# The prologue of an attention kernel rearranged: first batch's norm and queries alone, the mask loaded earlier, K's third part in halves

## The chip, the cores and the metric

The kernel runs on one core of one Trainium2 chip. The metric is the device time of one execution in microseconds, the median of several runs of the same program.

## What is computed

One transformer-like block over two batches of 256 query tokens of width 256: cross attention onto 4096 context keys (16 heads of 16), then a retention layer, then a small mixture of experts, each with a residual. Only the start of the cross attention matters here:

```python
q = split_heads(layernorm(x) @ w_q.T + b_q)          # 2 x 256 queries, 16 heads x 16
k = split_heads(ctx @ w_k.T + b_k)                   # 2 x 4096 keys
v = split_heads(ctx @ w_v.T + b_v)
scores = einsum('bhqd,bhkd->bhqk', q, k) / 4
scores = where(mask, -inf, scores)                   # mask: 1x1x256x4096, the same for both batches
attn = einsum('bhqk,bhkd->bhqd', softmax(scores), v)
x1 = x + attn @ w_o.T + b_o
```

The mask hides all but the last 896 keys or so, plus a part of the first block of these. The kernel works on these 7 blocks of 128 keys (`KB`), and checks from the whole mask that nothing else is shown. If something is, a general path with a loop over windows runs; it does not run with these inputs.

## The kernel before

**Precision by parts.** Queries and keys are float32, each split into three bfloat16 parts (high, middle, low): `hi = bf16(v)`, `rest = v - hi`, `mid = bf16(rest)`, `low = rest - mid`. Six products of parts (`K_PART`, `Q_PART`) stand below one another in the contraction: `kstack` and `qstack` have 6 x 16 = 96 rows for each head. They are filled by DMAs from SBUF to SBUF, six for each piece: three of K's high part, two of its middle, one of its low part and so for the queries, in another order. Rows 96 to 98 (`MROW:KROWS`) hold ones in `kstack` and the maximum, in three parts, in `qstack`, so that scores come out with the maximum subtracted. One DMA writes the ones, `kstack<-onesb` (L365), three rows of 57,344 bytes in pieces of 1,024.

**Pieces.** `n = 2b + f`: batch b, half f of the heads. `k0` to `k3` are K's four pieces of 128 x 896, `q` has the same four of 128 x 256. The kernel before makes the queries of both batches in one go (L589 to L598: transposes of four normed tiles, matmuls 512 columns wide).

**Stages and steps.** A stage is one batch and 4 heads (8 stages, `STAGES`). Each has 8 maximum tiles (`max_tile`, L656): a product of 128 queries and 896 keys on TensorE (L678, two halves, and L683 for the mask), whose maximum VectorE takes (L1461). Tiles use two pairs of PSUM banks in turn, so tile m waits until the maximum of tile m-2 is taken (`take_pair`). After a stage's 8th tile the maxima are split (L1480 to L1483), turned by TensorE (`turn_rows`, L699), copied by ScalarE (L1120) and loaded into `qstack` by a DMA. The main loop (`steps`) has 56 steps, 7 to a stage: `scores` (L724, two halves), exp on ScalarE (L1147), `weighted` sums (L740) of the step before; tiles of later stages are spread over the steps (`TILE_STEP`). The first `FIRST_TILES` = 10 tiles come before the loop.

**The prologue, engine by engine.** The order on each is written out by hand, and each engine takes its instructions strictly in order.

- SP issues loads: x (512 KB), w_k, the first batch's context in halves, w_q, w_v, then `kstack<-onesb`, then K's first piece and the middle and low parts of the first query piece to the stacks, then the two halves of the mask (512 KB each), the second context, and the other pieces.
- TensorE: 34 warm-up matmuls (68 records of L579), `keys(0)`, transposes, `queries()`, `keys(1)`, `values(0)`, `values(1)`; tile 0 (waits for `qstack` and `kstack`), `values(2)`, tile 1, `values(3)`, then tiles 2 to 9 with 3 warm-up matmuls behind each of tiles 2 to 6; `odd_late` (L995, sums of the late mask, behind tile 7); rows of stage 0; `odd_early` (L1001) with a last product of ScalarE's sums (L1004); `keys(2)`; the steps.
- VectorE: the norm of four tiles (L1366 to L1355), K(0)'s rest and its middle and low parts, the same for the first query piece, the rest of the second, the rest of K(1), and the maxima.
- ScalarE: evacuates PSUM (K's and the queries' high parts, the values), issues three `qstack` DMAs, sums the early mask (L1279: 3200 and 1600 columns), copies the rows, issues their DMA, forms the flag for the fast path (L1284, L1286) and copies K(2) in halves (L1100).
- GpSimd: constants, middle and low parts of the second queries (L490, L492), casts of the mask (L498, L499), K(1)'s low part (L503), then K(2) and K(3) in full (`keys_cut`: L516, L520, L524, L528).

## Time and profile before

| what | us |
|---|---|
| median of 3 runs | 248.17 (248.14 to 249.93) |
| the profiled execution, whole | 248.6 |
| its span (first to last instruction) | 246.8 |
| tile 0 starts | 26.34 |
| first scores (step 0) start | 43.15 |
| last of the 56 steps ends, about | 150 |

The profile is of one execution. Its times are microseconds from the start of its span. PE is TensorE's matmuls, PEld its weight loads, DVE VectorE, ACT ScalarE, POOL GpSimd, SP SyncE; a float32 matmul has two records. "Idle before" and the releaser behind "<-" say how long an engine stood before an instruction and what ended that. The granted clock of TensorE is given as a share of full speed, the DMA share as the mean busy share of the core's 16 DMA engines.

### The profile page before, as it was taken

The page shows a single profiled execution, that of the slowest core. Times are in us where ns is not written, and L with a number is a line of the kernel's source. Part 1 is how long each engine was busy: PE and PEld are TensorE (multiplying, and loading weights), DVE is VectorE, ACT ScalarE, POOL GpSimd, SP SyncE. Part 2 cuts the span into 40 slices and gives each one's busy share as a digit, 9 for nine tenths or more (in the row PEclk, how much of TensorE's full clock was granted, in tenths as well). Part 3 has the DMA queues.
Part 4 walks back from the last instruction along what each step waited for, and adds up shares of the span by engine and source line. Part 5 has one row for each costly group of instructions (what it writes and reads, how often), then busy time and mean ns, then how long its engine had stood idle before and what let it go on. Part 6 is the DMA issues. An engine that isn't in the chain of part 4 may idle for free.

```text
span 246.8 us, 3909 instructions
## 1 busy us (share of the span) xinstructions
PE 228.2 (92%) x1454; PEld 127.7 (52%) x1454; DVE 149.2 (60%) x340; ACT 111.6 (45%) x234; POOL 25.0 (10%) x28
## 2 busy tenths in 40 slices
PE   7979998999999999999999898989898889899892
PEld 7846684444565645454544433534746763635340
DVE  1656494893836748787876063485457538586682
ACT  2143463565747567777777784323144041201000
POOL 7002340805400400000000000000000000000000
PEclk9999999999999999999999999999999999999999
DMA  6659996909008800460000000000000000000000
GB/s 198 201 128 222 341 228 119 335 6 227 1 0 203 230 4 0 114 230 1 3 4 3 1 3 0 0 1 0 3 0 0 0 1 3 1 0 21 23 28 25
DMA packets 14541, 17.94 MB, mean 73 GB/s; under 512 B 2468, under 2 KB 13620, under 8 KB 14516
## 3 DMA queue, kind: packets, MB, share of 16 engines
q1 hardware_dynamic: 13220, 17.28, 25.5%
q10 hardware_dynamic: 1295, 0.34, 0.9%
q8 instruction: 14, 0.23, 0.4%
q14 instruction: 12, 0.09, 0.1%
HBM read 9.79 MB, written 0.52 MB: 42 GB/s over the span
## 4 chain that ended last, share of the span: by engine, by line
PE 70%; DVE 18%; ACT 5%; issue 3%; DMA 2%; SPq 0%; POOL 0%; DVEq 0%; ACTq 0%; POOLq 0%
PE bank L740 10%; PE bank L724 9%; PE bank L923 8%; PE bank L678 8%; DVE cneg L1461 7%; PE bank L830 6%; PE bank L579 4%; PE bank L633 4%; PE bank L640 4%; PE bank L903 3%; PE bank L791 3%; DMA qstack<-xbo 2%; ACT prob L1147 2%; PE bank L811 1%; PE bank L728 1%
## 5 line engine op out<-in xcount | busy, mean ns | idle before, releaser
L1461 DVE TENSOR_REDUCE cneg<-bank 128x1 f32<-128x896 f32 x64 | 68.2, 1088 | 33.1 <-PE bank L678 33.0
L1147 ACT ACTIVATE prob<-bank 128x512 f32<-128x512 f32 x112 | 65.6, 598 | 25.5 <-PE bank L724 17.0
L724 PE MATMUL bank<-qstack,kstack 99*128 99x256 bf16 x224 | 42.3, 274 | 1.7 <-ACT k_full L1100 0.8
L678 PE MATMUL bank<-kstack,qstack 96*128 96x448 bf16 x128 | 38.6, 354 | 0.8 <-DMA qstack<-xbo 0.4
L740 PE MATMUL bank<-prob,vals 128*32 128x256 f32 x448 | 35.8, 391 | 0.4 <-ACT prob L1147 0.4
L724 PEld LDWEIGHTS bank<-qstack,kstack 99*128 99x128 bf16 x224 | 17.5, 97 | 25.5 <-issue 12.1
L830 PE MATMUL bank<-w_late,xnT 128*128 128x512 f32 x48 | 22.0, 595 | 0.3 <-ACT xnT L1176 0.3
L678 PEld LDWEIGHTS bank<-kstack,qstack 96*128 96x128 bf16 x128 | 12.5, 98 | 9.6 <-DVE cneg L1461 1.7
L923 PE MATMUL bank<-ctxT,xnT 128*128 128x512 f32 x32 | 17.1, 616 | 0.3 <-DVE x_in L1641 0.3
L1641 DVE SCALAR_TENSOR_TENSOR x_in<-bank,nwts,x_in 128x256 f32<-128x256 f32 x32 | 15.5, 484 | 2.5 <-PE bank L923 1.4
L923 PE MATMUL bank<-kpart,xnT 128*128 128x512 f32 x32 | 16.3, 592 | 0.0
L740 PEld LDWEIGHTS bank<-prob,vals 128*32 128x32 f32 x448 | 8.8, 108 | 14.1 <-issue 11.1
L579 PE MATMUL bank<-ones 128*128 128x128 f32 x98 | 13.5, 297 | 1.5 <-POOL ones L481 1.4
L683 PE MATMUL bank<-hide_q,identb 128*128 128x128 bf16 x64 | 14.0, 219 | 0.0
L579 PEld LDWEIGHTS bank<-ones 128*128 128x128 f32 x98 | 13.1, 211 | 1.8 <-POOL ones L481 1.4
L640 PE MATMUL bank<-wv,ctxT 128*128 128x256 f32 x56 | 13.1, 383 | 0.2
L830 PEld LDWEIGHTS bank<-w_late,xnT 128*128 128x128 f32 x48 | 8.5, 190 | 8.2 <-issue 7.7
L633 PE MATMUL bank<-ctxT,wk 128*128 128x448 f32 x32 | 12.8, 542 | 0.0
L1176 ACT ACTIVATE xnT<-bank 128x256 f32<-128x256 f32 x8 | 3.0, 384 | 19.7 <-PE bank L791 19.7
L640 PEld LDWEIGHTS bank<-wv,ctxT 128*128 128x128 f32 x56 | 10.5, 190 | 2.3 <-DVE cneg L1461 0.7
L1500 DVE COPY acc<-bank 128x136 f32<-128x136 f32 x8 | 2.4, 299 | 13.0 <-PE bank L707 12.6
L923 PEld LDWEIGHTS bank<-kpart,xnT 128*128 128x128 f32 x32 | 6.1, 190 | 7.7 <-issue 7.7
(142 smaller groups left out, 260.4 us busy)
## 6 DMA issues: line engine op xcount, KB each, us to landing
kstack<-kpart SPq DMA_DIRECT2D x24, 224.0 KB, 4.5
w_late<-in_w_ret SPq DMA_DIRECT2D x1, 1536.0 KB
mask_all<-in_mask SPq DMA_DIRECT2D x2, 512.0 KB, 6.0
ctxT<-in_w_exp SPq DMA_DIRECT2D x1, 1024.0 KB
kpart<-in_w_exp SPq DMA_DIRECT2D x1, 1024.0 KB
ctxT<-in_ctxT SPq DMA_DIRECT2D x2, 448.0 KB, 6.2
ctxT<-in_ctxT SPq DMA_DIRECT2D x1, 896.0 KB, 9.4
qstack<-acc SPq DMA_DIRECT2D x6, 128.0 KB, 6.4
```

The costliest lines, as they stand in the source:

```text
L579: pe.matmul(bank[:, where, 0:P], ones[:, :], ones[:, :], start=True, stop=True)
L633: mm = pe.matmul(bank[:, banks + h, 0:HC], wk[:, i, f * P:(f + 1) * P], ctxT[:, b, i, h * HC:(h + 1) * HC], start=(i == 0), stop=(i == KIN ...
L640: mm = pe.matmul(out[:, (k - blocks[0]) * D:(k - blocks[0] + 1) * D], ctxT[:, b, i, k * P:(k + 1) * P], wv[:, i, :], start=(i == 0), stop= ...
L678: mm = pe.matmul(out, qstack[0:MROW, h, b, qt * P:(qt + 1) * P], kstack[0:MROW, b, h, half_ * HC:(half_ + 1) * HC], start=True, stop=not h ...
L683: pe.matmul(out[:, 0:P], identb[:, :], hide_q0[:, qt, :], start=False, stop=True, skip_group_check=True)
L724: mm = pe.matmul(out[:, hh * NQ:(hh + 1) * NQ], kstack[0:KROWS, b, h, kt * P:(kt + 1) * P], qstack[0:KROWS, h, b, :], start=(hh == 0 or no ...
L740: mm = pe.matmul(bank[32 * j:32 * j + PADV, OB, 0:NQ], vals[:, b, kt, e:e + PADV], prob[:, (2 * u + j // 2) % PROBS, (j % 2) * NQ:(j % 2 + ...
L830: mm = pe.matmul(bank[:, 2 + m, :], xnT[:, c, t * P:(t + 1) * P], w_ret[:, c, m * 512:(m + 1) * 512], start=(c == 0), stop=(c == KIN - 1))
L923: mm = pe.matmul(bank[:, PAIR_BANKS[m % 4], :], xnT[:, c, t * P:(t + 1) * P], w_exp[c][:, 2 * pr:2 * pr + 2, :], start=(c == 0), stop=(c = ...
L1147: act.activation(prob[:, n % PROBS, :], bank[:, S0 + jj, :], ACT.Exp).then_inc(c["prob_ready"], 1)
L1461: dve.tensor_reduce(cneg[:, st % 2, i:i + 1], bank[:, pair:pair + 2, 0:HC], AXXY, ALU.max, negate=True).then_inc(c["max_read"], 1)
L1641: dve.scalar_tensor_tensor(x_in[:, t, :], src, nwts[:, t, e:e + 1], x_in[:, t, :], ALU.mult, ALU.add).then_inc(s["pair_read"], 1)
```

## The change

It touches only what runs before step 1, on all five engines.

- `WARM_UP` 34 becomes 14; the warm-up matmuls between tiles go. `FIRST_TILES` is 12, so steps 0 and 1 hold two tiles each and step 2 none (before, steps 0 to 2 held two each).
- SP loads x in two halves (the second behind w_q), and both halves of the mask right behind w_v, ahead of `kstack<-onesb` and of all stack copies. The other query pieces are stacked one at a time, each by six DMAs: piece 1 before K(1), pieces 2 and 3 after it.
- VectorE norms batch 0, splits K(0) and the 256 columns of query piece 0, then norms batch 1. It splits nothing more.
- ScalarE copies the other pieces (queries 1 to 3, K(1)) out of PSUM in float32, with their bias, and GpSimd makes all three parts of each, four operations a piece. GpSimd's order: mask casts, query piece 1, K(1), query pieces 2 and 3, then as before.
- TensorE makes queries of batch 1 between tiles 2 and 5, then `odd_late`, tile 6, `odd_early`, tile 7, half of K(2), the rows, tiles 8 and 9, the other half, tiles 10 and 11. `odd_early` is now ahead of the rows.
- ScalarE sums the early mask behind `queries_out(2)` and `(3)`, which wait for q_ready 4; the flag for the fast path comes before the rows, K(2)'s first half between flag and rows. The first scores wait for K(2)'s halves apart (`k2_half` and k_taken 2).

The diff, cut to its core; `c.key(name, n)` is `c.at` with K(0)'s semaphores apart, since other engines now count for the later pieces.

```diff
-WARM_UP, KEEP_WARM = 34, 3
+WARM_UP = 14
-FIRST_TILES = 10
+FIRST_TILES = 12
...
-            sp.dma_start(x_in[:, :, :], a["x"].rearrange("(t p) c -> p t c", p=P)).then_inc(s["x_loaded"], 16)
+            load_x(0, s["x_loaded"])
...
             sp.dma_start(wq[:, :, :], a["wq"].rearrange("(c p) n -> p c n", p=P)).then_inc(s["wq_loaded"], 16)
+            load_x(1, s["x_second"])
             sp.dma_start(wv[:, :, :], a["wv"].rearrange("(c p) n -> p c n", p=P)).then_inc(s["wv_loaded"], 16)
+            for t in range(QT):
+                sp.dma_start(mask_all[:, t, :], a["mask"][t * P:(t + 1) * P, :]).then_inc(mask_loaded[t], 16)
             sp.wait_ge(s["const_ready"], 1)
             sp.dma_start(kstack[MROW:KROWS, :, :, :].rearrange("r b h k -> r (b h k)").rearrange("r (n k) -> r n k", k=512),
                          onesb[:, :].unsqueeze(1).to_broadcast([3, NB * NH * CH // 512, 512])).then_inc(s["ones_loaded"], 16)
...
             stack_keys(only, 0)
-            stack_queries(0, 0, (1, 2))
-            for t in range(QT):
-                sp.dma_start(mask_all[:, t, :], a["mask"][t * P:(t + 1) * P, :]).then_inc(mask_loaded[t], 16)
+            stack_queries(0, ((None, 0), ("q0_mid", 1), ("q0_cut", 1)))
             load_ctx(1, slice(0, CH), only["ctx_loaded1"])
-            stack_keys(only, 1, (0, 1))
-            stack_second_queries()
-            stack_queries(0, 1, (0, 1, 2))
-            stack_keys(only, 1, (2,))
+            stack_queries(1, (("q_hi", 1), ("q_mid", 1), ("q_cut", 1)))
+            stack_keys(only, 1)
+            for n in (2, 3):
+                stack_queries(n, (("q_hi", n), ("q_mid", n), ("q_cut", n)))
...
+            def queries_cut(n):
+                b, f = divmod(n, KIN)
+                full, part = q_rest[:, n, :], qparts[f][:, :, b * NQ:(b + 1) * NQ]
+                pool.wait_ge(s["q_taken"], n)
+                pool.tensor_copy(part[:, 0, :], full).then_inc(s["q_hi"], 1)
+                pool.wait_ge(s["q_hi"], n)
+                pool.tensor_tensor(full, full, part[:, 0, :], ALU.subtract).then_inc(s["q_rested"], 1)
+                pool.wait_ge(s["q_rested"], n)
+                pool.tensor_copy(part[:, 1, :], full).then_inc(s["q_mid"], 1)
+                pool.wait_ge(s["q_mid"], n)
+                pool.tensor_tensor(part[:, 2, :], full, part[:, 1, :], ALU.subtract).then_inc(s["q_cut"], 1)
+
+            queries_cut(1)
+            keys_cut(only, 1)
+            queries_cut(2)
+            queries_cut(3)
...
-            for m in range(FIRST_TILES):
-                max_tile(only, m)
-                if m < 2:
-                    values(only, m + 2)
-                elif m < ODD_AT:
-                    if m == 2:
-                        pe.wait_ge(*only.at("v_evac", NVP))
-                    warm_up(KEEP_WARM, OB)
-                elif m == ODD_AT:
-                    odd_late()
+            pe.wait_ge(s["wk_loaded"], 16)
+            keys(only, 0)
+            turn_first(0)
+            queries(0)
+            queries(1)
+            keys(only, 1)
+            values(only, 0)
+            values(only, 1)
+            max_tile(only, 0)
+            values(only, 2)
+            max_tile(only, 1)
+            values(only, 3)
+            max_tile(only, 2)
+            turn_first(1)
+            max_tile(only, 3)
+            queries(2)
+            max_tile(only, 4)
+            queries(3)
+            max_tile(only, 5)
+            pe.wait_ge(*only.at("v_evac", NVP))
+            odd_late()
+            max_tile(only, 6)
+            odd_early()
+            max_tile(only, 7)
+            keys_half(only, 2, 0)
             turn_rows(only, 0)
-            odd_early()
-            keys(only, 2)
+            max_tile(only, 8)
+            max_tile(only, 9)
+            pe.wait_ge(s["q_taken"], 3)
+            keys_half(only, 2, 1)
+            max_tile(only, 10)
+            max_tile(only, 11)
...
-            turn_out()
-            queries_high(0)
-            queries_high(1)
+            turn_out(0)
+            queries_high()
+            queries_out(1)
+            keys_out(only, 1)
             act.wait_ge(s["const_ready"], 4)
-            values_out(only, 0)
+            for n in range(NVP):
+                values_out(only, n)
+            turn_out(1)
+            queries_out(2)
+            queries_out(3)
...
-            rows_out(only, 0)
-            act.wait_ge(*only.at("mrows_ready", 1))
-            act.dma_start(qstack[MROW:KROWS, 0:G, 0, :], mrows[:, 0, :]).then_inc(only["mrows_loaded0"], 16)
             act.wait_ge(s["odd_summed"], 1)
...
-            keys_out(only, 2)
+            keys_half_out(only, 2, 0)
+            rows_out(only, 0)
+            act.wait_ge(*only.at("mrows_ready", 1))
+            act.dma_start(qstack[MROW:KROWS, 0:G, 0, :], mrows[:, 0, :]).then_inc(only["mrows_loaded0"], 16)
+            keys_half_out(only, 2, 1)
...
+            def first_layernorm(b):
+                tiles = range(QT * b, QT * b + QT)
+                dve.wait_ge(s["x_second" if b else "x_loaded"], 16)
+                for t in tiles:
+                    pre(dve.bn_stats(stats[:, t, :], x_in[:, t, :]), t == tiles[-1])
+                normalize("dve_pre", x_in, tiles, "xn_ready", scale=DK ** -0.5)
```

## Rows read from the trace of the kernel before

**Rows 1.** The page: busy time of TensorE, and two of its costliest groups.

```profile
PE 228.2 (92%) x1454; PEld 127.7 (52%) x1454; DVE 149.2 (60%) x340; ACT 111.6 (45%) x234; POOL 25.0 (10%) x28
...
L1461 DVE TENSOR_REDUCE cneg<-bank 128x1 f32<-128x896 f32 x64 | 68.2, 1088 | 33.1 <-PE bank L678 33.0
...
L640 PE MATMUL bank<-wv,ctxT 128*128 128x256 f32 x56 | 13.1, 383 | 0.2
```

**Rows 2.** The chain that ended last, 0 to 62 us: start, us, what.

```profile
21.01 5.28 DMA qstack<-xbo
...
26.34 0.36 PE bank L678
```

**Rows 3.** Timeline of VectorE, 0 to 68 us: start, us busy, line, operation, count [idle before].

```profile
31.86 5.54 DVE L1461 TENSOR_REDUCE cneg<-bank 128x1 f32<-128x896 f32 x5 [0.31 <-PE bank L678]
...
44.23 6.22 DVE L1461 TENSOR_REDUCE cneg<-bank 128x1 f32<-128x896 f32 x6 [4.14 <-PE bank L678]
```

**Rows 4.** Timeline of TensorE, 0 to 62 us.

```profile
26.79 1.89 PE L640 MATMUL bank<-wv,ctxT 128*128 128x256 f32 x8
...
28.96 1.03 PE L640 MATMUL bank<-wv,ctxT 128*128 128x256 f32 x4
...
38.25 0.85 PE L1001 MATMUL bank<-w_late,signs 128*1 128x200 bf16 x8
...
39.06 3.27 PE L633 MATMUL bank<-ctxT,wk 128*128 128x448 f32 x8
43.15 0.38 PE L724 MATMUL bank<-qstack,kstack 99*128 99x256 bf16 x2 [0.82 <-ACT k_full L1100]
...
53.62 0.39 PE L724 MATMUL bank<-qstack,kstack 99*128 99x256 bf16 x2
```

**Rows 5.** Stretches: us, busy us (instructions) by engine, granted TensorE clock, DMA share, GB/s.

```profile
10.00:15.00 5.00, 4.56 (x23) 2.79 (x21) 1.87 (x4) 1.69 (x4) 0.00 (x0) 1.00 0.20 27
15.00:15.50 0.50, 0.00 (x0) 0.00 (x0) 0.47 (x2) 0.50 (x2) 0.00 (x0) 1.00 0.07 10
16.00:25.00 9.00, 9.00 (x29) 5.29 (x29) 4.64 (x6) 2.98 (x4) 1.77 (x2) 1.00 1.09 234
25.00:26.30 1.30, 0.95 (x5) 0.49 (x3) 0.00 (x0) 0.31 (x1) 0.00 (x0) 1.00 1.03 377
26.30:28.60 2.30, 2.26 (x12) 1.87 (x13) 1.09 (x1) 1.11 (x2) 0.00 (x0) 1.00 0.99 378
```

**Rows 6.** Timeline of SyncE, which issues most DMAs, 0 to 70 us.

```profile
4.01 0.96 SPq L365 DMA_DIRECT2D kstack<-onesb  x1
14.39 4.64 SPq L375 DMA_DIRECT2D kstack<-kpart  x6
```

**Rows 7.** DMA issues by line: count, KB each, median us to landing.

```profile
kstack<-kpart SPq DMA_DIRECT2D x24, 224.0 KB, 4.5
...
mask_all<-in_mask SPq DMA_DIRECT2D x2, 512.0 KB, 6.0
...
kstack<-onesb SPq DMA_DIRECT2D x1, 168.0 KB
```

**Rows 8.** Timeline of ScalarE, 0 to 68 us.

```profile
30.29 2.87 ACT L1279 ACTIVATE w_late<-mask_all 128x3200 bf16<-128x3200 uint8 x1
...
34.58 0.19 ACT L1279 ACTIVATION_READ_ACCUMULATOR w_late<-mask_all 128x1 f32 x1
...
38.84 1.30 ACTq L1282 DMA_DIRECT2D qstack<-mrows  x1
```

**Rows 9.** Timeline of GpSimd, 0 to 68 us.

```profile
44.08 1.89 POOL L520 TENSOR_TENSOR k_full<-k_full,kpart 128x896 f32<-128x896 f32 x1
```

**Rows 10.** Stretches, the warm-up matmuls (L579) alone; columns as in rows 5.

```profile
1.50:4.00 2.50, 2.50 (x12) 2.50 (x13) 1.00 0.68 187
5.00:9.50 4.50, 4.50 (x42) 4.50 (x42) 1.00 1.00 334
```

**Rows 11.** Timeline of TensorE, 0 to 62 us, its longest pause before tile 0.

```profile
15.82 3.67 PE L597 MATMUL bank<-xnT,wq 128*128 128x512 f32 x8 [1.25 <-ACT xnT L1076]
```

258 lines of the change are left out of this document (125 added, 133 removed).

## The prediction

> **What bounds the kernel now.** I read the page first. TensorE is busy for 228.2 of 246.8 us [rows 1], but that is an average over stages, so the next view is the chain that ended last, cut to the first 62 us, which is all that the change touches. It runs through the warm-up matmuls, K's first part and the queries, and then through 5.28 us of DMA: tile 0 starts at 26.34, when the last piece of `qstack` lands [rows 2]. From there the tiles go at VectorE's pace, five maxima in 5.54 us, 1.11 each [rows 3], TensorE being fed warm-up matmuls in between. K's third part and its ScalarE copy end the prologue, and the first scores start at 43.15 [rows 4]. So two stretches count: start to tile 0 (26.3 us), and tile 0 to first scores (16.8 us).
>
> What sets 26.34? The windows show the DMA engines by stretch [rows 5]. From 10 to 15 us they are busy for 0.20 of 16, so about three engines, at 27 GB/s; in the next half microsecond 0.07 of 16, one engine. Nothing is outstanding then but `kstack<-onesb` (168 KB, issued at 4.01) [rows 6, 7]: its outer dimension has three rows, and it runs on three engines only. The stack copies (6 of 224 KB for K [rows 7], 6 of 64 KB for the queries, 1.77 MB) follow it in SP's queue, issued from 14.39 [rows 6]. At the 234 GB/s of 16 to 25 us they need 7.6 us on 16 equal engines, so from 15.6 they should be in by about 23.2. Yet the last lands at 26.3, while the window 25 to 26.3 already moves 377 GB/s, the rate of loads from HBM: most engines have gone on to the mask, and a few are still behind with the stack. I read these as the engines that `onesb` held longest: about 10 to 16 us, then the stack, no rest in between. It is an inference, since the view does not name engines.
>
> **The change, part by part.**
>
> *First batch alone.* The norm of two tiles instead of four saves VectorE some 1.5 us, half of its statistics and of its outputs, and x's first half lands up to 0.7 us sooner (256 KB at 377 GB/s). 20 of 34 warm-up matmuls go, some 4 us of TensorE work; K(0) then waits for its context instead, which the DMA engines deliver by 8.6 or so. Its second half takes 1.5 us (half of the 3.27 for eight records [rows 4]), to 10.1, and ScalarE's copy of it ends some 1.2 later. The queries have 256 columns, not 512. So the stack copies can be issued at about 11.4 instead of 14.39. SP needs 4.64 us for the six of K [rows 6] and 0.6 for each of the queries' three, the last of them at about 17.3 instead of 21.0. This is 3 to 4 us of gain, if the DMA engines can take them.
>
> *Mask ahead of the stack.* SP now issues both mask loads (2 x 512 KB) before `onesb`. For 13 engines the time is idle. But in SP's queue they also stand in front of `onesb` on its three engines. 1.05 MB at 377 to 378 GB/s [rows 5] is 2.8 us, so `onesb` starts near 12.8 instead of 10, and its slowest engine ends it near 19 instead of 16. Earlier issues cannot help that engine: it had no rest before, and has 2.8 us more to do. Tile 0 then starts at 26.3 + 2.8 = **29.1**: **+2.8 us**. Lower bound: these engines, alone after the others are done, work at HBM's pace (377/16 = 23.6 GB/s each instead of 14.6), so 110 KB take 4.7 us and not 7.6, tile 0 at about 26. Below that only if the reading is wrong (22, below). Upper: `onesb` slows beside the stack copies, +1 us.
>
> The Trainium skill, DMA: Bandwidth & Descriptors, section "Why a DMA increments its semaphore by 16 and not by 1", has the rule that a transfer uses the largest number of engines, up to 16, that divides the slowest dimension of both patterns; for three rows that is three. The section "Queues, rings and completion order" says each engine takes a queue's descriptors in ring order. The 0.20 of 16 agrees, and by these two the mask stands in front of `onesb`, whose engines' share of the stack waits for both.
>
> *Tile 0 to first scores.* TensorE's order, start to start at its full pace: tile 0.44, values(2) 1.73, tile, values(3) 0.87 (26.79 to 28.96 is values(2) and a tile [rows 4]); then tile 2, four transposes (0.5), tile 3 once ScalarE has copied them (0.7 wait), queries(2) 0.87, tile 4, queries(3) 0.87. From tile 0 this is 7.4 us: 29.1 to 36.5. VectorE (1.09 a tile [rows 1]) keeps up, being fed slower than that. Tile 5, `odd_late`, tile 6 and `odd_early` follow (2.3 us, 38.8). Here a wait appears. `odd_early` ends with a product that needs ScalarE's early sums, and ScalarE now makes them behind `queries_out(2)` and (3), which wait for q_ready 4. These two take 0.8 and the sums 30.29 to 34.77, 4.5 us [rows 8]: 36.5 + 0.1 + 0.8 + 4.5 = 41.9. So **TensorE stands for 3.1 us in front of tile 7**, and tiles 7 to 11, both halves of K(2) and the rows are queued behind it. Before, the sums were done at 34.8 and needed at about 39: this cover is gone. Then: product and tile 7 to 42.5, half of K(2) 1.5 (3.27 for both [rows 4]), rows once tile 7 is reduced 0.5, tiles 8 and 9 0.9, second half 1.5, tiles 10 and 11 0.9: 47.8. mrows (issue 1.30 [rows 8]) are in by then, and the ScalarE copy of the second half lies under tiles 10 and 11. First scores at about 47.9, 18.8 us after tile 0 where it was 16.8: **+2.0 us**. The ScalarE copy that is now hidden (it ended the prologue before, 0.82 of wait at 43.15 [rows 4]) and the two tiles more are in this sum.
>
> *Steps 0 to 4.* They ran 43.15 to 53.62 [rows 4], 10.5 us, paced in part by six maxima in a row (6.22 us, after VectorE stood 4.14 [rows 3]). Now four tiles instead of six are left, but tiles 8 to 11 come just ahead and VectorE starts with a backlog: maxima from 45.1 on end with tile 15 near 54.2, so step 3 starts there. Steps 3 and 4 then save a wait or two: 9.9 us, **-0.6 us**.
>
> *GpSimd.* Its queue: mask casts (data from about 13), query part 1, K(1), parts 2 and 3. A 896-wide subtraction takes 1.89 [rows 9], K(1)'s four operations 5.9 and a query part about 2.1, a total near 41 after q_taken 3 at 37.4; the first exp that needs it comes near 48. Nothing. K(1) reaches `kstack` by about 41, needed at step 3 (54). Nothing; if the cover were gone it would be 1 us for each query part.
>
> *TensorE's clock.* After values(1), near 20.3, TensorE has no work until 29.1: nearly 9 us. In the records, the first warm-up matmuls come at 12 in 2.5 us and later at 42 in 4.5, about half the rate, with the granted clock given as 1.00 in both [rows 10]. So an array that had been idle works at half its rate at first, 1.2 against 2.4 GHz. The pauses of before (1.25 us [rows 11]) cost nothing. A stretch at half rate of the same length as at the start, some 2.5 to 3 us, costs 1.2 to 1.5 us, at tile 0, where TensorE sets the pace: I take **+1.2**, between 0 and 1.5. The Trainium skill, TensorE: Matmul & The Clock Gate, Part 1, says that an idle array falls back to 1.2 GHz; no row of before has so long a pause later on, so none shows it.
>
> Sum: 2.8 + 2.0 - 0.6 + 1.2 = **+5.4 us**. The profiled execution was 248.6 (span 246.8 and 1.8 around it), the median 248.17; the difference is put on the median: **253.5 us**. All after step 5 is the same code, shifted.
>
> **Rivals.**
> A. *The intended gain.* `onesb` isn't what holds the last pieces. Then the stack copies run from 12.8 for 8.7 us, tile 0 at 22.0, no long pause and no clock loss: +5.4 - 1.2 - 7.1 = -2.9, **245.3 us**. For: earlier issues on every engine. Against: the 0.20 and 0.07 shares and the 377 GB/s before the last landing. Even so the wait for the early sums takes most of the gain.
> B. *The held engines catch up* once they have the fabric to themselves: tile 0 at 26, +5.4 - 3.1 = +2.3, and with a shorter clock loss about +1.8, **250.0 us**. Against: `onesb` was slow with all engines idle (27 GB/s on three, 9 each), so copies inside SBUF aren't quickened by quiet.
> C. *The clock stays up*: 253.5 - 1.2 = 252.3 us, inside the likeliest's own range.
> It decides at tile 0: for no change at all it would have to start near 24.9 (29.1 less 5.4 and with 1.2 given back).
>
> **How the numbers follow.** The likeliest, 0.70: 253.5, with its own range 251.8 to 255.5 (clock 0 to 1.5, tile 0 at 28.4 to 30.1). B 0.17, A 0.13. The range, to leave out A and little more: 249.6 to 255.5. A measurement of this kernel tells about 1% from no change, 245.7 to 250.7. Faster 0.10 (A, most of it), same 0.17 (B, most, and A's upper part), slower 0.73.
>
> **What would show it.** Right: the first L678 matmul near 29 after an idle time of some 8 us released by the DMA of `qstack`; a DMA share near 0.2 or with a tail of few engines until about 19; TensorE idle some 3 us before L1004, released by ScalarE's accumulation; the first L724 near 48 to 49; L640's matmuls behind tile 0 well above their mean of 383 ns [rows 1]. Wrong: the first L678 near 22 (then A), or the early sums done before `odd_early` asks for them, or first scores before 44.

## The result, and the profile after

| what | before, us | after, us |
|---|---|---|
| median | 248.37 (4 runs) | 261.11 (260.1 to 262.24, 4 runs) |
| the profiled execution, whole | 248.6 | 261.27 |
| its span | 246.8 | 259.3 |
| its mean granted clock | 1.00 | 0.96 |
| tile 0 starts | 26.34 | 28.59 |
| first scores start | 43.15 | 55.21 |
| step 5 starts | 53.62 | 66.43 |

The change makes the kernel slower: ratio 1.0499, interval 1.0446 to 1.0551. The direction was forecast, the size was not: 261.1 lies 5.6 us above the upper end of 255.5. The spans differ by 12.5 us, and all of it is there at step 5 (66.43 - 53.62 = 12.8). Behind step 5 both kernels run alike, to within 0.3 us.

TensorE's timeline of after; the columns are start, us busy, line, operation, count and, in brackets, the idle time before with its releaser. L699 to L704 are the tiles, L647 is K(2), L747 the scores:

```profile
17.66 2.75 PE L660 MATMUL bank<-wv,ctxT 128*128 128x256 f32 x12
28.59 0.56 PE L699 MATMUL bank<-kstack,qstack 96*128 96x448 bf16 x1 [8.18 <-DMA qstack<-xbo]
...
29.42 3.62 PE L660 MATMUL bank<-wv,ctxT 128*128 128x256 f32 x8
...
34.50 0.35 PE L699 MATMUL bank<-kstack,qstack 96*128 96x448 bf16 x1
...
43.95 0.19 PE L1020 MATMUL bank<-early_sums,minus 128*1 128x2 f32 x2 [2.78 <-ACT w_late L1321]
...
44.90 2.83 PE L647 MATMUL bank<-ctxT,wk 128*128 128x448 f32 x4
...
48.76 1.67 PE L647 MATMUL bank<-ctxT,wk 128*128 128x448 f32 x4
...
50.95 0.35 PE L699 MATMUL bank<-kstack,qstack 96*128 96x448 bf16 x1
55.21 0.59 PE L747 MATMUL bank<-qstack,kstack 99*128 99x256 bf16 x2 [3.91 <-DMA qstack<-mrows]
...
66.43 0.39 PE L747 MATMUL bank<-qstack,kstack 99*128 99x256 bf16 x2
```

These rows answer [rows 4]. There are three brackets of some length where before had 0.39 and 0.82: 8.18 us before tile 0, 2.78 before the product of the early sums, 3.91 before the first scores. Behind each of them the same instruction takes longer than elsewhere: values(2) 3.62 us instead of 1.89, the first half of K(2) 2.83 where the second half takes 1.67, the scores 0.59 instead of 0.39. The windows say why (stretch, length, busy us of PE, PEld, DVE, ACT and POOL, granted clock, DMA share, GB/s):

```profile
12.50:15.00 2.50, 2.50 (x11) 1.79 (x10) 2.43 (x4) 0.47 (x1) 0.86 (x1) 1.00 0.51 121
15.00:18.00 3.00, 3.00 (x12) 1.94 (x11) 2.96 (x4) 0.00 (x0) 2.13 (x2) 1.00 0.53 108
...
28.50:33.00 4.50, 4.41 (x12) 3.24 (x13) 1.09 (x1) 0.00 (x0) 0.00 (x0) 0.50 1.11 204
34.00:41.50 7.50, 6.93 (x45) 4.45 (x43) 6.28 (x6) 3.77 (x5) 2.05 (x4) 1.00 0.30 71
43.00:46.50 3.50, 2.55 (x8) 1.44 (x9) 1.29 (x3) 1.82 (x5) 0.81 (x2) 0.62 0.41 101
52.00:55.00 3.00, 0.00 (x0) 0.00 (x0) 0.99 (x1) 0.00 (x0) 2.86 (x3) 0.84 1.01 406
55.20:61.00 5.80, 5.79 (x22) 3.02 (x22) 3.08 (x3) 2.27 (x4) 1.80 (x1) 0.51 0.10 34
```

Three times the granted clock is at 0.50 or 0.51, the lower level (1.2 GHz), and each time TensorE had stood before. (The row from 43 us says 0.62 since it begins inside the wait; from 43.9 to 47 the clock is 0.50.) The row of 52 to 55 us holds the third wait: TensorE and ScalarE do nothing, while the DMA engines are fully busy at 406 GB/s. What they move is in SP's timeline:

```profile
5.38 0.95 SPq L380 DMA_DIRECT2D kstack<-onesb  x1
11.39 9.12 SPq L390 DMA_DIRECT2D kstack<-kpart  x6
20.56 1.90 SPq L399 DMA_DIRECT2D qstack<-xbo  x3
...
48.62 0.39 SPq L408 DMA_DIRECT2D w_late<-in_w_ret  x1
```

and in the chain that ended last (start, us, what):

```profile
21.86 6.68 DMA qstack<-xbo
...
39.53 4.37 ACT w_late L1321 x4
...
48.67 6.45 DMA qstack<-mrows
```

The late weights, 2 MB, are issued at 48.62, the 6 KB of `mrows` at 48.67. The small transfer takes 6.45 us. The flag had been ready since 45.13; SP was busy with the copies of queries 2 and 3 until 47.26, and then came to the weights. In the kernel before the rows' DMA was issued at 38.84 [rows 8] and the weights only at 42.11, so the rows were in `qstack` before anybody asked.

The second thing in SP's timeline: the six issues of K's first piece take 9.12 us where before they took 4.64 [rows 6]. SP itself is held (and ScalarE too, whose three `qstack` issues take 4.55 us where before they took 2.08), and so the last query piece is issued at 21.86, later than in the kernel before (21.01 [rows 2]), although VectorE had its last part ready at 17.4 (below).

### The profile page after: what moved, and what is told of

It is laid out like the page before. It is cut to its first block, busy times and chain, and to the rows that moved or that the text cites. A ratio compares the mean times of both kernels' runs of the same rounds, so it can differ in the third digit from the quotient of the medians.

```text
span 259.3 us, 3817 instructions
## 1 busy us (share of the span) xinstructions
PE 227.7 (88%) x1392; PEld 125.4 (48%) x1392; DVE 155.2 (60%) x349; ACT 110.8 (43%) x236; POOL 33.4 (13%) x41
## 4 chain that ended last, share of the span: by engine, by line
PE 65%; DVE 12%; DMA 8%; ACT 7%; SPq 4%; issue 3%; DVEq 0%; ACTq 0%
PE bank L763 10%; PE bank L747 10%; PE bank L699 9%; PE bank L946 8%; PE bank L853 5%; PE bank L660 4%; SPq L390 3%; PE bank L926 3%; PE bank L647 3%; PE bank L814 3%; DMA qstack<-xbo 3%; DMA ctxT<-in_ctxT 3%; DMA qstack<-mrows 2%; DVE cneg L1504 2%; ACT prob L1192 2%
## 5 line engine op out<-in xcount | busy, mean ns | idle before, releaser
L699 PE MATMUL bank<-kstack,qstack 96*128 96x448 bf16 x128 | 41.2, 376 | 8.2 <-DMA qstack<-xbo 8.2
L747 PE MATMUL bank<-qstack,kstack 99*128 99x256 bf16 x224 | 43.1, 279 | 4.8 <-DMA qstack<-mrows 3.9
L747 PEld LDWEIGHTS bank<-qstack,kstack 99*128 99x128 bf16 x224 | 17.9, 99 | 28.5 <-issue 15.8
L699 PEld LDWEIGHTS bank<-kstack,qstack 96*128 96x128 bf16 x128 | 13.1, 103 | 17.3 <-DMA qstack<-xbo 8.6
L660 PE MATMUL bank<-wv,ctxT 128*128 128x256 f32 x56 | 14.8, 419 | 0.2
L704 PE MATMUL bank<-hide_q,identb 128*128 128x128 bf16 x64 | 14.7, 230 | 0.0
L647 PE MATMUL bank<-ctxT,wk 128*128 128x448 f32 x32 | 14.3, 583 | 0.3 <-DMA ctxT<-in_ctxT 0.3
L660 PEld LDWEIGHTS bank<-wv,ctxT 128*128 128x128 f32 x56 | 11.8, 213 | 2.7 <-DVE cneg L1504 0.8
L1155 ACT COPY vals<-bank 128x512 f32<-128x512 f32 (+3 forms) x6 | 4.0, 660 | 18.9 <-PE bank L660 18.9
L1544 DVE COPY acc<-bank 128x136 f32<-128x136 f32 x8 | 2.4, 299 | 13.0 <-PE bank L728 12.8
L647 PEld LDWEIGHTS bank<-ctxT,wk 128*128 128x128 f32 x32 | 6.4, 208 | 5.3 <-issue 4.2
```

Source lines behind the costliest of these rows:

```text
L647: mm = pe.matmul(bank[:, c.key_banks(n) + h, 0:HC], wk[:, i, f * P:(f + 1) * P], ctxT[:, b, i, h * HC:(h + 1) * HC], start=(i == 0), stop= ...
L660: mm = pe.matmul(out[:, (k - blocks[0]) * D:(k - blocks[0] + 1) * D], ctxT[:, b, i, k * P:(k + 1) * P], wv[:, i, :], start=(i == 0), stop= ...
L699: mm = pe.matmul(out, qstack[0:MROW, h, b, qt * P:(qt + 1) * P], kstack[0:MROW, b, h, half_ * HC:(half_ + 1) * HC], start=True, stop=not h ...
L704: pe.matmul(out[:, 0:P], identb[:, :], hide_q0[:, qt, :], start=False, stop=True, skip_group_check=True)
L747: mm = pe.matmul(out[:, hh * NQ:(hh + 1) * NQ], kstack[0:KROWS, b, h, kt * P:(kt + 1) * P], qstack[0:KROWS, h, b, :], start=(hh == 0 or no ...
```

## The experiments

Three causes lie on the table: the place of the mask and of `onesb` in SP's queue (tile 0), the place of the early sums in ScalarE's order (the 2.78), and the weights against the rows (the 3.91), each with its stretch of half clock. The rival to each is that the wait is an effect of something else, and would come back elsewhere when its supposed cause is gone. Kernel names below are those of the headings. Ratios are to the kernel before on the same chip, whose medians were 248.36 to 248.92.

### rows_first: the weights wait for the rows

```diff
             with sp.If(fast > 0):
+                sp.wait_ge(*only.at("mrows_loaded0", 16))
                 late_weights()
```

> One wait more: SP holds the 2 MB of late weights until the DMA of the first rows (mrows) has landed. In the changed kernel tile 11 ended near 51.3 and the first scores stood until 55.2 for that DMA, issued at 48.67, 50 ns behind the weights' first issue; TensorE's clock then fell to half until 61. Theory W (the rows wait behind the weights on the DMA engines): rows in by about 50.3, first scores at 51.6, no spell at half clock after them, steps 0 to 2 paced by VectorE instead: about 5.5 us less, 255.6 us. Rival (the wait is ScalarE's issue and a DMA's own latency of 6 us): first scores stay near 55, 261 us.

Measured 256.54 us, ratio 1.0322 (1.0288 to 1.0356). TensorE's timeline:

```profile
52.22 0.38 PE L748 MATMUL bank<-qstack,kstack 99*128 99x256 bf16 x2 [0.24 <-issue]
```

The wait of 3.91 us is gone, the first scores start 3.0 earlier, and the granted clock is 1.00 from 52 to 58 us. So the rows' DMA did wait for the weights. Steps 0 to 4 now take 9.4 us (52.22 to 61.58) instead of 11.2: 1.9 us is the price of the third stretch of half clock, and a wait and its clock leave together. Step 5 starts 4.85 earlier: 3.67 of wait, 1.86 in the steps and 0.46 ahead of the early sums, less 1.14 for a longer second stretch of half clock (8.5 us from the sums' product to the last tile, 7.35 in after), which this edit doesn't touch.

### sums_early: the early sums behind the second values

```diff
-            for n in range(NVP):
-                values_out(only, n)
+            values_out(only, 0)
+            values_out(only, 1)
+            for t, n in enumerate((EARLY, EARLY // 2)):
+                act.wait_ge(mask_loaded[t], 16)
+                act.activation(unread[:, t * EARLY:t * EARLY + n], mask_all[:, t, 0:n], ACT.Copy, accum_out=early_sums[:, t:t + 1]).then_inc(s["early_summed"], 1)
+            values_out(only, 2)
+            values_out(only, 3)
             turn_out(1)
             queries_out(2)
             queries_out(3)
```

The same loop behind `queries_out(3)` goes.

> ScalarE makes the early mask sums behind the second values' copy (from about 21, where it is idle until 33) instead of behind the last queries. Theory: TensorE no longer stands 2.8 us before L1020, no half clock at 43 to 47 (1.6 us more); the fast flag comes 4.4 us sooner, while SP is still issuing query stack copies until 47.3, so the rows' DMA gets ahead of the late weights and the 3.9 us wait and its half clock go as well: about 10.5 us less in all, 250.6 us. Rival (the weights still stand ahead of the rows): only 4.4 us less, 256.7 us.

Measured 252.48, ratio 1.0149 (1.0121 to 1.0178). The one edit removes both waits:

```profile
41.48 0.19 PE L1020 MATMUL bank<-early_sums,minus 128*1 128x2 f32 x2
...
44.66 0.28 PE L720 MATMUL bank<-identb,mpart 128*12 128x128 bf16 x2 [0.94 <-DVE mpart L1528]
...
48.78 0.38 PE L747 MATMUL bank<-qstack,kstack 99*128 99x256 bf16 x2 [0.48 <-issue]
```

ScalarE issues the rows at 45.36, 3.3 us earlier, while SP is busy with the stack copies of queries 2 and 3 as before and issues the weights only at 49.08. So the late sums caused the second wait and, by bringing the rows' issue and the weights' together, the third. From the sums' product to the last tile it takes 6.8 us, of which 0.94 is a wait: 5.9 us of work at full clock, against 7.35 without a wait in after. So the second stretch of half clock added 1.5 us of work, but TensorE would have waited 0.94 us for the maxima in any case: it made the path only 0.5 us longer (7.35 against 6.8). In rows_first, where the stretch is longer, it is 1.7 (8.5 against 6.8).

### ones_late and mask_back: what holds tile 0

ones_late moves the one DMA of `onesb` behind the stack copies that tile 0 needs:

```diff
-            sp.wait_ge(s["const_ready"], 1)
-            sp.dma_start(kstack[MROW:KROWS, :, :, :].rearrange("r b h k -> r (b h k)").rearrange("r (n k) -> r n k", k=512),
-                         onesb[:, :].unsqueeze(1).to_broadcast([3, NB * NH * CH // 512, 512])).then_inc(s["ones_loaded"], 16)
...
             stack_keys(only, 0)
             stack_queries(0, ((None, 0), ("q0_mid", 1), ("q0_cut", 1)))
+            sp.wait_ge(s["const_ready"], 1)
+            sp.dma_start(kstack[MROW:KROWS, :, :, :].rearrange("r b h k -> r (b h k)").rearrange("r (n k) -> r n k", k=512),
+                         onesb[:, :].unsqueeze(1).to_broadcast([3, NB * NH * CH // 512, 512])).then_inc(s["ones_loaded"], 16)
```

> The DMA of ones into kstack (three rows, about three of 16 engines) is issued behind K's and the queries' first stack copies instead of ahead of them; the mask stays where the change put it. Theory R (ones hold three engines, the stack copies' shares on them wait, and SP's issue stalls with them, one issue of 4.2 us): six K issues from 11.4 take 4.6 us again and not 9.1, tile 0 near 22 instead of 28.6, TensorE idle under 2 us before it, so no half clock there (2.4 us): 9 us less, 252.1 us. Rival (the DMA engines together are the bound, or the mask's own packets): tile 0 stays at 28 to 29, 261 us.

mask_back puts the two mask loads where they were, behind the same stack copies, and leaves `onesb` in front:

```diff
-            for t in range(QT):
-                sp.dma_start(mask_all[:, t, :], a["mask"][t * P:(t + 1) * P, :]).then_inc(mask_loaded[t], 16)
...
             stack_queries(0, ((None, 0), ("q0_mid", 1), ("q0_cut", 1)))
+            for t in range(QT):
+                sp.dma_start(mask_all[:, t, :], a["mask"][t * P:(t + 1) * P, :]).then_inc(mask_loaded[t], 16)
```

> Both mask loads go back behind the first query piece's stack copies, as in the kernel before; ones stay ahead of the stack copies, all else as changed. Theory R: ones start near 10 and not 12.8, so tile 0 comes 2.5 to 3 us sooner, near 26; the idle time before it is some 5.5 us, half clock still but shorter. GpSimd's mask casts then come at 28 and hold up its query and K pieces, which have room. The flag for SP comes late as before the rows, so the weights may fall behind the rows' DMA: 252 us if they do, 258 if they do not. Rival (the mask's place costs nothing on ones' engines): tile 0 at 28.6.

Measured: ones_late 252.88, 1.0141 (1.0077 to 1.0204); mask_back 253.46, 1.0201 (1.0148 to 1.0253). TensorE's timeline of ones_late:

```profile
21.98 0.36 PE L699 MATMUL bank<-kstack,qstack 96*128 96x448 bf16 x1 [1.29 <-DMA qstack<-xbo]
27.16 0.36 PE L699 MATMUL bank<-kstack,qstack 96*128 96x448 bf16 x1 [1.53 <-DVE cneg L1504]
36.62 0.19 PE L1020 MATMUL bank<-early_sums,minus 128*1 128x2 f32 x2 [2.79 <-ACT w_late L1321]
...
47.32 0.59 PE L747 MATMUL bank<-qstack,kstack 99*128 99x256 bf16 x2 [3.35 <-DMA qstack<-mrows]
```

and of mask_back:

```profile
26.10 0.55 PE L699 MATMUL bank<-kstack,qstack 96*128 96x448 bf16 x1 [5.50 <-DMA qstack<-xbo]
```

The two terms of the prediction's reading come apart. The mask in front of `onesb` costs 28.59 - 26.10 = 2.5 us, forecast 2.8. `onesb` in front of the stack copies costs 28.59 - 21.98 = 6.6 with the mask ahead of it. SP issues K's six copies in 4.09 us in ones_late, 6.16 in mask_back, 9.12 in after: its stalls go with the transfer in front. But the cost is not gone in ones_late, it is handed on. From 22 to 28 us the DMA engines are fully busy (share 1.04) and move 112 GB/s, and SP needs 8.50 us for the six copies of query piece 1. And in ones_late the other two waits, 2.79 and 3.35, are there as in after.

The last of them says more about the rows and the weights. In ones_late ScalarE issues the rows first:

```profile
41.34 1.30 ACTq L1329 DMA_DIRECT2D qstack<-mrows  x1
41.61 0.39 SPq L405 DMA_DIRECT2D w_late<-in_w_ret  x1
```

A lead of 0.27 us at the start of the issue did not help them. Their issue takes 1.30 us and the weights' 0.39, so it ended later; that this is the reason was not tested.

mask_back has no third wait: SP is late with its copies there and issues the weights at 49.41, 3.7 us behind the rows (45.71), and the first scores start at 49.01. That is why it is 7.7 us faster than after, with only 2.5 of it at tile 0.

### all_three and pool_waits: the edits together

all_three is ones_late, sums_early and rows_first in one. pool_waits adds a wait of GpSimd for the second norm, ahead of its casts of the mask:

```diff
+            pool.wait_ge(s["xn_ready"], TT)
             for t in range(QT):
```

> ones behind the first stack copies, early sums behind the second values' copy, late weights behind the first rows: the three edits of ones_late, sums_early and rows_first together. Theory (three separate waits, each with its own half clock): from ones_late's 252.9 us the 2.8 us before L1020 and some 1.7 of half clock go, and the 3.35 us before the first scores and some 2.6 of half clock, less what VectorE's pace takes back: 243.5 us, faster than the kernel before. Rival (the same gain counted twice, since sums_early alone already moved the rows ahead of the weights): 248 us.

> all_three, and GpSimd waits for the second norm (xn_ready 4) before its mask casts. In the changed kernel VectorE's cast of query 0 took 1.45 us and its subtraction 1.62 beside GpSimd's casts, the two norm outputs 2.86; in mask_back, where GpSimd was idle then, 0.29, 0.42 and 0.73. Theory P (VectorE's operations from SBUF to SBUF wait out GpSimd's): all are short again, VectorE is done at about 19 instead of 26, the last query copies are issued earlier, tile 2 no longer waits for VectorE: 2 us less than all_three, 241.5 us. Rival (GpSimd's later start holds up K(1) or the mask sums): no gain or a loss, 243.5 us or more.

Measured: all_three 247.69, 0.9943 (0.9911 to 0.9975), pool_waits 247.44, 0.9929 (0.9895 to 0.9963). That is barely faster than before (0.6 and 0.7%), and some 4 and 6 us above what was expected. In all_three (the profiled execution took 248.83 us) tile 2 waits, and then the rows, though the weights are issued after them (43.80):

```profile
27.47 0.36 PE L700 MATMUL bank<-kstack,qstack 96*128 96x448 bf16 x1 [2.25 <-DVE cneg L1507]
...
43.88 0.38 PE L748 MATMUL bank<-qstack,kstack 99*128 99x256 bf16 x2 [1.82 <-DMA qstack<-mrows]
```

Behind each of these two waits the granted clock is 0.50 (28 to 30 us, 45 to 48 us). Tile 2 waits for a maximum that stands in VectorE's queue behind the second norm, and the norm ends at 26.42 only, where in mask_back it ended at 19.12. VectorE's timeline of after:

```profile
14.30 1.45 DVE L1435 CAST xbo<-prob 128x256 bf16<-128x256 f32 x1
15.78 1.62 DVE L1437 TENSOR_TENSOR xbo<-prob,xbo 128x256 bf16<-128x256 f32 x1
...
22.26 2.86 DVE L1398 TENSOR_SCALAR xn<-x_in,moments,nw 128x256 f32<-128x256 f32 x2
```

of mask_back, where the mask isn't there yet and GpSimd rests:

```profile
14.49 0.29 DVE L1435 CAST xbo<-prob 128x256 bf16<-128x256 f32 x1
14.81 0.42 DVE L1437 TENSOR_TENSOR xbo<-prob,xbo 128x256 bf16<-128x256 f32 x1
...
18.39 0.73 DVE L1398 TENSOR_SCALAR xn<-x_in,moments,nw 128x256 f32<-128x256 f32 x2
```

and GpSimd's in after, at the same time:

```profile
14.14 1.46 POOL L499 CAST w_late<-mask_all 128x1536 bf16<-128x1536 uint8 x1 [9.23 <-DMA mask_all<-in_mask]
15.54 1.58 POOL L500 CAST w_late<-mask_all 128x1600 bf16<-128x1600 uint8 x1
```

In all_three the norm's two outputs take only 0.74 us together, and it is the small steps before them that are slow. This one, of two columns, takes 0.16 in pool_waits; beside it is what GpSimd does at the time:

```profile
20.93 1.74 DVE L1387 TENSOR_TENSOR nw<-nw 128x2 f32<-128x2 f32 x1
20.77 1.88 POOL L517 TENSOR_TENSOR k_full<-k_full,kpart 128x896 f32<-128x896 f32 x1
```

They end at 22.67 and 22.65. So even a VectorE instruction of two columns can be held until GpSimd's ends.

In after, VectorE's cast of 256 columns ends at 15.75, about when GpSimd's of 1536 does (15.60), and the subtraction at 17.40, behind GpSimd's second (17.12). In pool_waits the three instructions are back to 0.29, 0.43 and 0.73, the norm ends at 18.78, and tile 2 doesn't wait. Yet the kernel is no faster:

```profile
22.06 0.36 PE L701 MATMUL bank<-kstack,qstack 96*128 96x448 bf16 x1 [1.80 <-DMA qstack<-xbo]
...
33.88 1.77 PE L649 MATMUL bank<-ctxT,wk 128*128 128x448 f32 x4 [1.10 <-DMA ctxT<-in_ctxT]
...
42.98 0.38 PE L749 MATMUL bank<-qstack,kstack 99*128 99x256 bf16 x2 [3.75 <-DMA qstack<-mrows]
```

The rows are issued 2.5 us earlier than in all_three (36.60 and 39.12) and arrive 0.9 earlier: they now fall among the stack copies of K(1) and of queries 2 and 3. From 34 to 40 us the DMA share is 1.06. What was won in front of the DMA engines' backlog is given back in it; that it is these copies that the rows meet is an inference, which rows_clear below bears out.

### kept_warm: no rest before tile 0

```diff
             values(only, 1)
+            pe.wait_ge(*only.key("k_taken", 1))
+            warm_up(44, S0)
             max_tile(only, 0)
```

> The changed kernel with 44 warm-up matmuls (7.7 us) between values(1) and tile 0, into the two PSUM banks that K(1) has left; nothing else. Theory C (the stretch at half clock behind tile 0 comes from the 8 us of idle TensorE before it and costs 2.4 us): tile 0 still at 28.6, granted clock 1.00 there, tile 2 at 32 instead of 34.5: 2.4 us less, 258.7 us. Rival (those matmuls wait for something else, such as DMA traffic or VectorE): 261 us.

Measured 255.03, ratio 1.0221 (1.0174 to 1.0267), 3.7 us less than expected. The granted clock is 1.00 from 28 to 34 us, and tile 0 to tile 2 takes 3.5 us (30.22 to 33.70) instead of 5.9 (28.59 to 34.50): the first stretch of half clock cost 2.4, as this run was to tell. Its warm-ups end late, so that tile 0 starts 1.6 later. The surprise is at the other end: the first scores start at 51.87 without a wait. SP issues the weights at 48.73, the rows are issued at 48.24. The rows are 0.49 us ahead, and that was enough; 0.05 us behind (after) and 0.27 ahead (ones_late) were not. So half a microsecond between the two decided on 4 us and on the third stretch of half clock. It is the same effect as in rows_first, met by chance.

### before_ones: the kernel before with `onesb` later

The same DMA moved in the kernel before, nothing else:

```diff
-            sp.wait_ge(s["const_ready"], 1)
-            sp.dma_start(kstack[MROW:KROWS, :, :, :].rearrange("r b h k -> r (b h k)").rearrange("r (n k) -> r n k", k=512),
-                         onesb[:, :].unsqueeze(1).to_broadcast([3, NB * NH * CH // 512, 512])).then_inc(s["ones_loaded"], 16)
...
             load_ctx(1, slice(0, CH), only["ctx_loaded1"])
+            sp.wait_ge(s["const_ready"], 1)
+            sp.dma_start(kstack[MROW:KROWS, :, :, :].rearrange("r b h k -> r (b h k)").rearrange("r (n k) -> r n k", k=512),
+                         onesb[:, :].unsqueeze(1).to_broadcast([3, NB * NH * CH // 512, 512])).then_inc(s["ones_loaded"], 16)
```

> The kernel before with one edit: the DMA of ones is issued behind the second batch's context instead of ahead of the first stack copies. Theory R (in the kernel before too, tile 0 waits for the three engines that ones held): tile 0 at about 24.3 instead of 26.3, all behind it follows: 2 us less, 246.3 us. Rival (all 16 engines are the bound there): tile 0 at 26.3, 248.3 us.

Measured 252.05, ratio 1.0128 (1.0099 to 1.0157): 3.2 us longer, where a gain of 2 was expected. The profiled execution took 250.12 us and the other three 251.68 to 252.52, so the trace shows less than half of this. Tile 0 starts at 26.98, with no idle time before it. In the kernel before TensorE itself is busy until 25.95 (26.34 less the 0.39 of idle time), and here its warm-ups, the same 68 records, end at 11.88 (1.43 and 10.45) instead of 10.68 (1.43 and 9.25). So in the kernel before, TensorE's own work and the DMA of `qstack` end within 0.4 us of one another, and taking `onesb` from the front could gain no more than that. Later it stands in the way: five issues of K take 9.72 us, and

```profile
44.85 0.38 PE L724 MATMUL bank<-qstack,kstack 99*128 99x256 bf16 x2 [1.88 <-DMA qstack<-mrows]
```

So in that order of the work `onesb` stands better ahead of all stack copies than at the one other place that was tried. From 12 to 14 us, where the kernel before had a DMA share of 0.20 and 25 GB/s, this run has 0.00: what those few engines carried was indeed `onesb`.

### after_spread and spread_all: `onesb` on more engines

Three DMAs of one row each in place of one of three rows, in after, and in after with sums_early and rows_first:

```diff
-            sp.dma_start(kstack[MROW:KROWS, :, :, :].rearrange("r b h k -> r (b h k)").rearrange("r (n k) -> r n k", k=512),
-                         onesb[:, :].unsqueeze(1).to_broadcast([3, NB * NH * CH // 512, 512])).then_inc(s["ones_loaded"], 16)
+            for r in range(3):
+                sp.dma_start(kstack[MROW + r:MROW + r + 1, :, :, :].rearrange("r b h k -> r (b h k)").rearrange("r (n k) -> r n k", k=512),
+                             onesb[r:r + 1, :].unsqueeze(1).to_broadcast([1, NB * NH * CH // 512, 512])).then_inc(s["ones_loaded"], 16)
```

> The changed kernel with the DMA of ones cut into three, one row each (56 pieces of 1 KB), at the same place in SP's queue: by the notes' rule on the slowest dimension each then runs on 14 engines instead of 3. Theory R (three engines held by ones are what makes tile 0 late and SP's issue slow): the ones take about 1.2 us of each engine, SP's six K issues 4.6 us again, tile 0 near 23, no half clock behind it; VectorE, slowed by GpSimd, then ends its second norm only at 25 and takes back 1 us: 7 us less, 254 us. Rival (the mask's bytes ahead of the stack, not the ones' engines): tile 0 stays near 28, 261 us.

> Ones in three row DMAs at the changed kernel's place, early sums earlier, late weights behind the first rows. In all_three the ones, though later, still held three engines: SP stood 9.7 us in six query issues instead of 3.8, pieces 1 to 3 came late and the rows' DMA (issued 39.1) met them, 1.8 us of wait. Theory: with ones spread SP runs free, tile 0 at 23, first scores near 40.4 without a wait for the rows: 245 us. Rival (the stack copies of pieces 1 to 3 themselves meet the rows' DMA): a wait for mrows of 2 to 4 us stays, 247.5 us.

Measured: after_spread 261.04, 1.0494 (1.0422 to 1.0567), the same as after; spread_all 252.64, 1.0163 (1.0113 to 1.0214). Tile 0 starts at 27.92 and 28.14. The windows of after_spread, beside those of after above and, last, one of the kernel before, where `onesb` has the engines to itself:

```profile
12.50:15.00 2.50, 2.50 (x11) 1.79 (x10) 2.40 (x6) 0.47 (x1) 0.00 (x0) 1.00 0.96 69
15.00:18.00 3.00, 3.00 (x12) 1.94 (x11) 2.59 (x16) 0.83 (x2) 0.00 (x0) 1.00 1.00 102
...
13.00:14.00 1.00, 1.00 (x7) 0.61 (x6) 0.67 (x1) 0.27 (x1) 0.00 (x0) 1.00 0.20 25
```

Nearly twice the share of the engines is busy (0.96 for 0.51) and they move fewer bytes (69 GB/s for 121). Both windows hold copies of K beside `onesb`, and the view does not tell them apart, so the rate of `onesb` itself when it is spread is not known. But alone, about three engines (0.20 of 16) moved 25 GB/s. If their number were the limit, 15 would move 125 (an estimate from this row), and the ones would be out of the way in under 2 us. Instead 69 GB/s is all that the busy engines move, K's bytes included. So the number of engines isn't what makes `onesb` slow; more of them are only held longer, and SP's six issues of K still take 7.88 us. The transfer reads and writes three partitions only; whether that is the reason, and whether the reading or the writing limits it, was not told apart. spread_all, at 252.64, also shows that sums_early and rows_first together are worth no more than sums_early alone (252.48): that one had put the rows ahead of the weights.

### best: more cover for TensorE, `onesb` still in front

spread_all with one product moved on TensorE, and GpSimd's casts later:

```diff
             values(only, 1)
-            max_tile(only, 0)
             values(only, 2)
+            max_tile(only, 0)
...
+            pool.wait_ge(s["xn_ready"], TT)
             queries_cut(1)
             keys_cut(only, 1)
+            for t in range(QT):
+                pool.wait_ge(mask_loaded[t], 16)
+            pool.tensor_copy(shown_late[:, :, :], mask_all[:, :, (FIRST + 1) * P:NKEY]).then_inc(s["odd_ready"], 1)
+            pool.tensor_copy(hidden_early[:, :], mask_all[:, 1, EARLY // 2:EARLY]).then_inc(s["odd_ready"], 1)
```

> spread_all, and: values(2) ahead of tile 0 on TensorE, GpSimd waits for the second norm and makes query piece 1 and K(1) before its mask casts. Theory P and the idle TensorE before tile 0: VectorE free at about 19 and not 26, tile 2 without its wait (1 us), 1.3 us of work moved into the idle time: 243 us. Rival (the later GpSimd work meets the rows' DMA, or odd_late waits for the casts): no better than spread_all.

Measured 249.77 (10 runs), 1.0042 (1.0014 to 1.007). It gains 2.9 on spread_all and stops there, with tile 0 at 28.29 behind a wait of 6.42 us. This is the one long wait that is left, and in ones_late tile 0 started at 21.98 with `onesb` behind the first stack copies: so `onesb` in front of them is what most probably keeps this kernel level with before.

### rows_clear: each transfer behind what is needed before it

Taken from these: `onesb` as one DMA, behind the second context's load; the sums early; GpSimd and values(2) as in best; and SP's end of the prologue in order of need:

```diff
-            for n in (2, 3):
-                stack_queries(n, (("q_hi", n), ("q_mid", n), ("q_cut", n)))
             fast = is_fast(sp)
...
             with sp.If(fast > 0):
-                late_weights()
+                sp.wait_ge(*only.at("mrows_loaded0", 16))
+                for n in (2, 3):
+                    stack_queries(n, (("q_hi", n), ("q_mid", n), ("q_cut", n)))
                 load_rows(only, 1)
+                late_weights()
                 stack_keys(only, 2)
```

> all_three's edits with ones (one DMA again) behind the second context; GpSimd after the second norm, its mask casts behind K(1); values(2) ahead of tile 0; the stack copies of query pieces 2 and 3 (needed at step 17) and the late weights behind the first rows' DMA. In after_spread the ones filled 14 engines for 5 us at some 60 GB/s, as slow as on three, so they have to come behind what is urgent. Theory D (every microsecond lost is a transfer in front of a more urgent one): tile 0 near 22 with TensorE busy until then, no half clock, rows in within 3 us of issue since only K(1)'s copies are in flight, first scores near 38 instead of 43.2: 242 us. Rival (K(1)'s copies, held up by the ones, still meet the rows, or come too late for step 3): first scores 41 or a wait at step 3, 246 us.

Measured 243.01 (242.78 to 243.28, 5 runs), ratio 0.9754 (0.972 to 0.9787): faster than both kernels. TensorE's timeline:

```profile
17.81 4.26 PE L664 MATMUL bank<-wv,ctxT 128*128 128x256 f32 x19
21.91 0.35 PE L703 MATMUL bank<-kstack,qstack 96*128 96x448 bf16 x1
...
26.64 1.13 PE L622 MATMUL bank<-xnT,wq 128*128 128x256 f32 x4 [1.32 <-ACT xnT L1114]
...
34.74 0.28 PE L724 MATMUL bank<-identb,mpart 128*12 128x128 bf16 x2 [1.08 <-DVE mpart L1532]
...
38.87 0.38 PE L751 MATMUL bank<-qstack,kstack 99*128 99x256 bf16 x2 [0.48 <-issue]
```

In the prologue no wait of TensorE for a DMA is left, its longest idle time there is 1.32 us, and the mean granted clock is 0.997. SP is still slow behind `onesb` (8.81 us for six issues from 19.44), but nothing that is needed soon stands behind it. So the change's own idea, the first batch alone, does bring tile 0 forward by 4.4 us, once the transfers are in order. Several edits stand together here, and their shares were not measured apart. Against pool_waits (247.44) what is gone is above all the wait for the rows, 3.75 us there, and the stretch of half clock behind it.

## Why the prediction was off, step by step

The difference at step 5 is 12.8 us. By the prediction's terms:

| term | forecast | measured | from |
|---|---|---|---|
| tile 0 | +2.8 | +2.25 | 28.59 - 26.34 |
| clock behind tile 0 | +1.2 | +2.4 | kept_warm |
| tile 0 to scores, without clock and the rows' wait | +2.0 | +3.0 | 26.6 - 16.8 - 2.4 - 0.5 - 3.9 |
| clock behind the early sums | 0 | +0.5 | after 7.35, sums_early 6.8 |
| rows' DMA behind the weights | 0 | +3.9 | bracket, rows_first |
| steps 0 to 4 at full clock | -0.6 | -1.1 to -1.3 | rows_first 9.4, sums_early 9.1, before 10.5 |
| clock in steps 0 to 4 | 0 | +1.9 to +2.1 | 11.2 against these |

- **Tile 0** came out near, +2.25 for +2.8, and that the mask in front of `onesb` costs 2.5 of it is shown by mask_back. The way there was another than the text's, so that the number fits so well is in part luck. In the text the stack copies are issued by 17.3 and then wait on three held engines, alone at the end. In the run SP's own issues stall behind `onesb`, 9.12 us for six, which was in no term; the last query issue comes at 21.86; and from 22.5 to 28 us not a few engines but all are busy (1.04). Spread over nearly all engines, `onesb` made tile 0 as late (after_spread).
- **The wait for the early sums**: forecast 3.1 us in front of this product, measured 2.78. Right in place, releaser and size. Behind it the text had 5.9 us to the last tile; at full clock it took 6.8 (sums_early), with 0.94 of wait for the maxima's parts.
- **The rows' DMA** is the step that failed. The text wrote of `mrows` that they "are in by then" and gave their way to `qstack` no time, because there was room behind its issue. It didn't ask what else the same moment sets free. The flag for the fast path now comes before the rows, SP uses it to issue 2 MB of weights, and these were issued within 0.05 us of the rows, which then took 6.45 us. The rule to price every issue that a moved step passes was applied to the front of SP's queue and not to its end. It cost 3.9 us of wait, and with the half clock that follows some 5.8.
- **The clock** was priced once, for one stretch of 2.5 to 3 us as at the start. It was the right mechanism, mis-sized and not repeated: the first stretch lasted from 28.5 to beyond 33 and cost 2.4, and the text's own wait of 3.1 us should have had a clock term as well. Together 1.2 forecast, about 4.9 measured (2.4, 0.5 and 2.0). The Trainium skill, TensorE: Matmul & The Clock Gate, Part 1, says that an idle array falls back to 1.2 GHz; the granted clock of 0.50 behind the idle times of 8.18, 2.78 and 3.91 us agrees.
- **Steps 0 to 4**: the backlog of VectorE that the text feared hardly showed; at full clock they gain 1.1 to 1.3, not 0.6.
- **GpSimd: nothing** held for its own results. It did slow VectorE beside it, by 1.16 + 1.20 us in the query split. In after this is hidden behind the wait for tile 0's copies; in all_three, where it also slowed the second norm, it came out as 2.25 us of wait.
- Of the rivals, A (tile 0 near 22) is what happens in ones_late, and even there the kernel is slower than before by 1.4%: the two other waits outweigh it, of which the text had only one. (Its terms, 12.8 and 8.7, add to 21.5 and not 22.0.) B's condition was never met: from 22.5 to 28 us all engines are busy, so the held ones had nothing to themselves. C is contradicted by the clock.

Two things stay open. The single gains don't add: ones_late, sums_early and rows_first give back 8.2, 8.6 and 4.6 us, all three together 13.4. Part is counted twice (sums_early frees the rows too), part goes to the DMA backlog; the runs don't split these shares. And that SP's issues stall while the engines are half busy was seen in every run of the changed prologue with `onesb` ahead (6.2 to 9.2 us for K's first six, 3.9 to 4.1 without), but not explained.

## What to carry over

A load put into idle DMA time is free only if nothing urgent will stand behind it, on the queue or on the engines, and a slow transfer into few partitions belongs behind all that is needed soon. When a flag or wait is moved, list every issue that it releases and compare their sizes and times with the small transfer that is needed next; here rows that were issued 0.27 us ahead of 2 MB still waited for 3.35 us, and rows 0.49 us ahead did not wait. Every wait of TensorE that a forecast contains needs a clock term of its own, read from the granted clock behind a wait of like length; waits of about 2 us went either way here.

## What was not expected of the hardware

- 168 KB into three partitions go at 25 GB/s on three engines (before, share 0.20), and spreading them over nearly all engines doesn't help: share 0.96 and 69 GB/s, K's copies included, against 0.51 and 121 in after.
- A transfer of 6 KB (`mrows`) took 5.89 us and made TensorE wait 3.35 when another engine issued 2 MB 0.27 us after it (ones_late), and was in time when the 2 MB were issued 0.49 us after it (kept_warm). The runs show the two sides, not what decides between them.
- SP's time for six issues is 3.9 to 9.7 us: 3.94 in rows_clear, 4.64 before, 6.16 in mask_back, 9.12 in after for K's first piece, 9.73 in all_three for query piece 1 behind `onesb`.
- VectorE's float32 work from SBUF to SBUF beside GpSimd's casts: 0.29 to 1.45, 0.42 to 1.62, 0.73 to 2.86 us, and two columns 0.16 to 1.74 (all_three). Maxima from PSUM keep 1.09 (after, 39.13 and 40.42, beside GpSimd's work from 39.23 on).
- The same 68 warm-up records took 9.25 us in before and 10.45 in before_ones; how long TensorE stays at the lower level varies from run to run by a microsecond or more (in after the second stretch was over at 47, in rows_first and kept_warm only behind 49).
- Idle times of 1.32 us (rows_clear, granted clock 1.00 from 22 to 30), 1.53 (ones_late, 1.00 from 24 to 32), 1.80 (pool_waits, 1.00 from 22.4 to 26) and 1.88 (before_ones, 1.00 from 45 to 50) were followed by full clock; two in all_three, 2.25 and 1.82, by 0.50 (28 to 30 us, 45 to 48 us). So the length of the idle time alone does not tell which it will be.
